# Attention fused with a 1x1 convolution: the low part of the probabilities is taken from their copy in SBUF

## The reference

```
q = Wq x + bq;  k = Wk x + bk;  v = Wv x + bv        # x: (4, 256, 4096), q and k: (4, 32, 4096)
att = softmax(q^T k / sqrt(32))                       # (4, 4096, 4096), over the keys
out = gamma * (v att^T)
fused = Wf [out ; x] + bf                             # Wf: (256, 512)
```

## Time and profile before

| | us |
|---|---|
| median of 3 runs | 2214.78 (2214.52 to 2215.31) |
| profiled execution, first to last instruction | 2212.5 |
| PE busy | 2179.2 |
| DVE busy | 1667.1 |
| ACT busy | 1663.0 |
| POOL busy | 1296.2 |

### The profile page before, as it was taken

One profiled execution on the slowest core, in us unless ns is written; L12 is line 12 of the kernel. 1 busy time (PEld: TensorE's weight loads), 2 busy tenths in 40 slices (PEclk: granted clock), 3 DMA queues, 4 the chain that ended last, 5 costly groups with the idle time before them and its releaser, 6 DMA issues.

```text
span 2212.5 us, 30655 instructions
## 1 busy us (share of the span) xinstructions
PE 2179.2 (98%) x9808; PEld 1780.7 (80%) x9808; DVE 1667.1 (75%) x2063; ACT 1663.0 (75%) x1860; POOL 1296.2 (59%) x553
## 2 busy tenths in 40 slices
PE   8999999999999999999999999999999999999997
PEld 7888888888878888888787888888878888888886
DVE  5778888785777888887577788888757778888874
ACT  5677777778567777777856777777776777777786
POOL 0366666667136666666713666666670466666666
PEclk9999999999999999999999999999999999999999
DMA  2000000000200000000020000000001000000000
GB/s 92 1 1 10 28 9 9 9 0 10 76 1 1 10 28 9 9 9 0 20 67 2 1 10 28 9 9 9 9 20 58 1 1 10 9 9 9 9 10 19
DMA packets 18703, 35.25 MB, mean 16 GB/s; under 512 B 1488, under 2 KB 2256, under 8 KB 18640
## 3 DMA queue, kind: packets, MB, share of 16 engines
q1 hardware_dynamic: 18368, 34.35, 4.5%
q10 hardware_dynamic: 272, 0.07, 0.0%
HBM read 17.63 MB, written 16.78 MB: 16 GB/s over the span
## 4 chain that ended last, share of the span: by engine, by line
PE 96%; DVE 1%; issue 1%; ACT 1%; POOL 0%; DMA 0%; POOLq 0%; DVEq 0%; ACTq 0%
PE ps_o L421 62%; PE ps_s L373 11%; PE ps_m L268 9%; PE ps_s L261 6%; PE ps_o L261 4%; PE ps_m L305 1%; DVE lo L603 0%; PE ps_m L359 0%; PE ps_m L366 0%; PE ps_m L367 0%; PE ps_s L282 0%; PE ps_s L283 0%; POOL acc L791 0%; ACT probs L531 0%; DVE inv_sum L701 0%
## 5 line engine op out<-in xcount | busy, mean ns | idle before, releaser
L791 POOL TENSOR_TENSOR acc<-acc,probs 128x1024 f32<-128x1024 f32 x448 | 1090.2, 2433 | 580.5 <-ACT probs L531 580.5
L608 DVE TENSOR_REDUCE part_max<-ps_m 128x1 f32<-128x512 f32 (+1 forms) x1024 | 699.2, 687 | 267.2 <-PE ps_m L268 225.0
L528 ACT ACTIVATE hi<-ps_s 128x1024 fp32r<-128x1024 f32 x508 | 522.0, 1027 | 399.7 <-PE ps_s L373 399.7
L421 PE MATMUL ps_o<-hi,val_hi 128*128 128x512 f32 x2048 | 811.1, 396 | 1.5 <-DVE o_raw L726 1.1
L421 PE MATMUL ps_o<-hi,val_lo 128*128 128x512 f32 x2048 | 803.9, 393 | 0.0
L675 DVE TENSOR_TENSOR lo<-ps_s,hi 128x1024 fp32r<-128x1024 f32 x508 | 615.7, 1212 | 188.1 <-ACT ps_s L532 185.5
L421 PE MATMUL ps_o<-lo,val_hi 128*128 128x512 f32 x2048 | 610.2, 395 | 0.0
L532 ACT ACTIVATE ps_s<-ps_s 128x1024 f32<-128x1024 f32 x508 | 524.7, 1033 | 0.0
L531 ACT ACTIVATE probs<-ps_s 128x1024 f32<-128x1024 f32 x508 | 518.3, 1020 | 0.0
L421 PEld LDWEIGHTS ps_o<-hi,val_hi 128*128 128x128 f32 x2048 | 386.3, 189 | 93.5 <-DVE o_raw L726 7.4
L421 PEld LDWEIGHTS ps_o<-lo,val_hi 128*128 128x128 f32 x2048 | 387.7, 189 | 90.8
(11 more groups left out here) (79 smaller groups left out, 1314.3 us busy)
## 6 DMA issues: line engine op xcount, KB each, us to landing
xf<-x SPq DMA_DIRECT2D x32, 512.0 KB, 3.6
out<-conv SPq DMA_DIRECT2D x32, 512.0 KB, 2.8
conv<-wf2T SPq DMA_DIRECT2D x1, 256.0 KB, 4.0
conv<-wv SPq DMA_DIRECT2D x1, 256.0 KB, 4.3
conv<-wf1T SPq DMA_DIRECT2D x1, 256.0 KB, 4.7
conv<-wkqT ACTq DMA_DIRECT2D x1, 64.0 KB, 4.4
vec<-vectors SPq DMA_DIRECT2D x1, 3.0 KB, 4.1
```

Source lines behind the costliest of these rows:

```text
L421: last = nc.tensor.matmul(ps_o[:, c], v[:, 2 * t + h, c * P:(c + 1) * P], p[:, t % 2, h, :], start=(t == 0 and i in (0, len(lead[0]))), st ...
L528: nc.scalar.activation(hi[:, t % 2], banks, ACT.Exp, scale=SCALE).then_inc(p_hi_done, 1)
L608: nc.vector.reduce_max(part_max[:, i, bass.ds(c, 1)], ps_m[:, i % 2], AX_X).then_inc(m_free, 1)
L791: nc.gpsimd.tensor_tensor(acc[:], acc[:], probs[:, t % PB], ALU.add).then_inc(acc_done, 1)
```

## The change

The third exponential of each pair is left out, and with it the semaphore `exp_done`. VectorE subtracts `hi` from `probs` in SBUF, which GpSimd also reads, where it had subtracted it from the exponential in PSUM; it waits for `probs_done`.

```diff
@@ semaphores
-        s_ready, p_hi_done, probs_done, exp_done = sem("s_ready"), sem("p_hi_done"), sem("probs_done"), sem("exp_done")
+        s_ready, p_hi_done, probs_done = sem("s_ready"), sem("p_hi_done"), sem("probs_done")
@@ ScalarE, end of project
                     nc.scalar.activation(probs[:, 0], ps_s[:, 0:2], ACT.Exp, scale=SCALE).then_inc(probs_done, 1)
-                    act.sem_inc(exp_done, 1)
                     exp(b * CHUNKS, 1, None)
@@ ScalarE, exp
                 nc.scalar.activation(probs[:, t % PB], banks, ACT.Exp, scale=SCALE).then_inc(probs_done, 1)
-                nc.scalar.activation(banks, banks, ACT.Exp, scale=SCALE).then_inc(exp_done, 1)
@@ VectorE
             def split_p(B, t):
-                dve.wait_ge(exp_done, B * PAIRS + (t + 1))
-                nc.vector.tensor_tensor(lo[:, t % 2], ps_s[:, 2 * (t % 2):2 * (t % 2) + 2],
+                dve.wait_ge(probs_done, B * PAIRS + (t + 1))
+                nc.vector.tensor_tensor(lo[:, t % 2], probs[:, t % PB],
                                         hi[:, t % 2].bitcast(F32), ALU.subtract).then_inc(p_lo_done, 1)
```

## The result

The changed kernel takes 2423.23 us (median of 4 runs, 2420.13 to 2428.67) against 2214.65 us: 1.0945 times the time of before, 95% interval 1.0932 to 1.0959. 2388 us were predicted, with a range of 2290 to 2440. The profiled execution's span is 2418.3 us, 205.8 more than before.

A forecast was written before the change was run, and what follows sets the result against it. TensorE, busy 98% of the span, was taken to bound the kernel. Terms 89 + 52 + 24 + 8 = 173 us, added to the 2212.5 us span plus 2.3, gave 2388 us; range 2290 to 2440.

The forecast's parts named there:

- end of a middle block: Pairs 14 on into the next block: VectorE and GpSimd take turns, o_raw copy 3.71 us late; 24 times, 89 us.
- acc_lo at pair 2: Line 680 at pair 2 of the next block: acc_lo races GpSimd's add; middle taken, 24 x 2.15 = 52 us.
- rival 6: TensorE's clock drops to half speed after stalls, a dozen times; adds 36 us and more, over 2440 us; chance 0.03.
- last blocks and the end: Last block of each image (4 times): turns of 3.34 us against pairs of 3.24; about 6 us each, 24 in all.
- first blocks: Blocks without scaling or finish: between 0.5 and 3 us, taken as 2; 8 us in all.
- upper branch: GpSimd's add wins against acc_lo at pair 2: stalls of 1.7 and 2.15 us, 3.85 together; 2428 us if always.
- Steady pairs: Pairs with maxima: split ends at 708.48 instead of 707.75, margin 0.1 us, zero cost; 12 us kept for the range.
- rival 1: VectorE's split and GpSimd's adds take turns on SBUF; 2388 us, 2346 to 2428 by acc_lo's race; chance 0.60.
- rival 2: A VectorE instruction right behind another goes ahead of the waiting GpSimd one; 76 us lost, 2291 us; chance 0.23.
- Rival 3: TensorE's delays space VectorE and GpSimd apart; only the first 1.2 us per middle block stays; 2249 us; chance 0.07.
- rival 4: No price: the subtraction fits into GpSimd's pauses; 2215 us; chance 0.04.
- Rival 5: Faster: the 0.23 us wait for o_raw goes in 24 blocks, if the cast is quick too; 2209 us; chance 0.03.

The follow-up runs named there:

- acc_lo run: The changed kernel with acc_lo (split_acc, VectorE) moved in pair 2 from behind the third chunk_max to ahead of the split; 2321.97 us.
- the first experiment: The kernel before with only VectorE's subtraction moved to probs in SBUF, all three exponentials and the old wait kept; 2424.74 us.
- two-exponential kernels: The kernel before with two exponentials, VectorE still subtracting out of PSUM, GpSimd summing hi: 2232.85 us; adds at their old time 2206.31; also q_stat copy on ScalarE 2208.95.

## Why the prediction was right, term by term

The mechanism held: the split and its neighbours take turns with POOL, and TensorE pays at the two places that were named. The number owes something to luck, since the misses of the sum have both signs. The sizes, from the distances between the copies of o_raw (line 726 before, 724 after) in the two traces, and from the acc_lo run for the parting of the first two:

| term | predicted us | measured us |
|---|---|---|
| end of a middle block | 24 x 3.71 = 89 | 24 x 3.62 = 87 |
| acc_lo at pair 2 | 24 x 2.15 = 52 | 24 x 3.35 = 80 |
| clock | 0 (rival 6) | 15 x 1.55 = 23 |
| last blocks and the end | 24 | 14 |
| first blocks | 8 | 1 |
| sum | 173 | 205 |

(3.62 is 63.92 - 60.30; 3.35 is 67.27 - 60.30 - 3.62. The acc_lo run still has its late matmul in pair 3, so these 3.62 hold a part of the second row. Counted by the stalls of the changed kernel, from start to start of the matmuls, pairs 2 and 3 cost 1.6 + 2.15 = 3.75 us, 90 in all, and the end 6.97 - 3.75 = 3.2, or 77.) The "1" of the first blocks is net of the 3 us that the kernel before lost there to the clock and the changed one did not.

The terms that were too small are acc_lo, by 28 us or more, and the clock, which was put at nothing and cost 23. The race of acc_lo was called undecided by 0.04 us and priced in the middle; it is decided, in all middle blocks, for the add, which asks 0.06 us earlier. The prediction's upper branch had 3.85 us for that case, and the two stalls that it named are there: 1.7 and 2.15 us said, 1.32 and 1.89 read, 1.6 and 2.15 with the hidden part. In this clean repeating schedule the race was no coin: the 0.04 us of the forecast had the right sign 24 times of 24. Leaning on it would have given 2428 us for 2423, but that nearness would have been luck too: the missing 23 us of the clock against some 30 too many at the block's end, in the last blocks and in the first.

- Steady pairs: the split at 1.94 us was said, 1.96 is read; no stall, as taken.
- Turns (rival 1) against DVE keeping its place (rival 2): finish, asked for at 802.52, got in between splits 14 and 15, whose exponentials had long been there. That is rival 1. But fold, asked for at 809.12, did not get in between the cast and the next split: the split of 809.24 took its bare 1.21 us and fold ended 1.16 us behind it. The chain lost a link there, and a stall of 0.29 us for a maximum in pair 1 (0.28 to 0.31 in most blocks) came in that was not foreseen; the sum hid both.
- Rival 3 (the stalls heal) is refuted by the 24 blocks, rival 4 by the first experiment.
- Rival 5 was right about the wait for o_raw: with two exponentials and no collision it goes. It was wrong that the cast forbids it, and it priced the wait too high: a middle block gains 0.09 us by it, not 0.23.
- Rival 6 (the clock) was taken for unlikely and came, in 15 blocks. It was priced at about 3 us for each from the one case of before; here each cost 1.55.
- ACT's busy time fell by 463 us and not by 525, since consecutive exponentials overlap by about 0.1 us in the profile; the middle blocks grew to 67.3 and 68.8 us, where 66 were said.
- Last blocks: turns of 3.34 against pairs of 3.24 us were right in kind; entry and scaling cost less than the whole turns that were charged.

The Trainium skill's rule ("SBUF — State Buffer", Who interferes with whom) held as to which instructions block each other: none of the 508 splits out of PSUM took over 1226 ns in the kernel before, nor over 1228 in the two-exponential kernels, and the SBUF form was held in every trace that has it. That issue order decides held at pair 2, where 0.06 us settled it, but not behind the cast.

## What to carry to other kernels

Before moving an operand of VectorE from PSUM to SBUF, look at what GpSimd reads at that time: here a VectorE instruction with two SBUF inputs and GpSimd's adds out of SBUF took turns, and the profile showed the wait as duration, not as idle time. Price it not by the sum of the two engines' work, which had room here, but by walking the queues at the places where both are full; the instruction that stalls can be an old one pushed out of its gap, as acc_lo was. And a faster producer can do the same harm: letting the adds start one exponential earlier cost 27 us (2232.85 against 2206.31).

## What the runs showed of the hardware that was not expected

- TensorE's granted clock fell to half after two stalls of 1.3 and 1.9 us within 5 us (PE idle for 3.2 us there), in 15 of 24 middle blocks, and did not in the other nine, whose stalls are the same; what decides between them stays open. The first of the two stalls isn't needed: with the scaling behind the split 20 of the middle blocks have a stall of 1.84 to 1.89 us in pair 3 and none ahead of it, and the clock fell behind it in 12 of them. With stalls of 0.9 and 0.7 us at the block's end and none over 0.3 elsewhere (acc_lo ahead of the split) it fell in none.
- Back to back on VectorE, a split lets a waiting GpSimd instruction in behind it, while the cast with one SBUF input did not let fold in ahead of the next split. The kernel with the scaling behind the split shows the same with an add, in all its 24 middle blocks; in the rows below the add asks 0.24 us ahead of the split and ends 2.26 us behind it. No run was made to tell why.

```profile
778.35 2.61 DVE L682 CAST q_stat<-queries 96x512 fp32r x1
780.88 1.21 DVE L673 TENSOR_TENSOR lo<-probs,hi 128x1024 fp32r<-128x1024 f32 x1
...
780.64 3.71 POOL L790 TENSOR_TENSOR acc<-acc,probs 128x1024 f32<-128x1024 f32 x1
```

- A 128x1024 add on GpSimd of 2.40 us takes 1.29 and 0.47 us (medians) with a half and an eighth of the columns, not quite in proportion. On the mean they take 1.49 and 0.65 us, since some wait for VectorE.
